# First attention of a two-layer macaron block: row maxima in halves of the heads, row sums out of the weighted sum

## What is computed

```python
disp, val = x @ w_disp + b_disp, x @ w_val + b_val          # per head 16 numbers
strain = disp_win - disp[:, :, :, None, :]                  # 32 earlier places per token
bond_act = gelu(strain @ w_strain + b_strain + state @ w_state_i + state_win @ w_state_j + rel_emb @ w_pos)
bond_logits = (bond_act @ w_bond_out)[..., 0] + b_bond_out[0]
damage_act = gelu(strain @ w_damage + b_damage)
damage = sigmoid((damage_act @ w_damage_out)[..., 0] + b_damage_out[0])
weights = softmax(where(cmask, bond_logits - damage * 10.0, -inf), axis=-1)   # over 32 places
out = einsum('bntd,bntde->bnte', weights, val_win)          # reshaped, then @ w_cproj + b_cproj
```

## Time and profile before

| | |
|---|---|
| median of 3 runs | 3083.24 us (3081.63 to 3083.78) |
| the profiled execution | 3079.87 us |
| its span, first to last instruction | 3078.1 us |
| around the span | 1.8 us |
| a0 within the span | 606.9 to 1311.9 us, chunks from 651.4 to 1263.2 |
| busy in the whole span: PE, DVE, ACT, POOL | 92%, 55%, 51%, 43% |
| one middle batch of a0 (1026.9 to 1106.3, 79.4 us), busy: PE, DVE, ACT, POOL | 70.6, 71.1, 72.3, 69.6 us |

### The profile page before, as it was taken

The page is one execution under the profiler, slowest core; times in us unless marked ns, Lnnn a source line. Parts: engine busy times, 40 slices in busy tenths (PEclk is TensorE's granted clock), DMA queues, the critical chain, the costliest instruction groups (busy, mean ns, idle before and its releaser), DMA issues. The chain is left out here.

```text
span 3078.1 us, 54231 instructions
## 1 busy us (share of the span) xinstructions
PE 2825.6 (92%) x19419; PEld 2033.0 (66%) x19419; DVE 1696.4 (55%) x4655; ACT 1562.0 (51%) x2621; POOL 1325.5 (43%) x1315
## 2 busy tenths in 40 slices
PE   6899999878988898788999998999789999988999
PEld 5799999733444443468999996666446666655666
DVE  5411111279888888673111111776776666656766
ACT  1133333359999898412333332333267777783333
POOL 5444444369888888363444442000134434320000
PEclk9899999979999999869999998999889999999999
DMA  8199999712222111363999997000142343301000
GB/s 288 60 324 330 325 328 328 221 52 62 63 59 63 53 56 48 97 217 113 329 324 324 325 325 215 1 0 0 49 111 73 87 100 97 80 1 40 14 14 20
DMA packets 299088, 432.11 MB, mean 140 GB/s; under 512 B 21185, under 2 KB 249702, under 8 KB 295782
## 3 DMA queue, kind: packets, MB, share of 16 engines
q1 hardware_dynamic: 273462, 394.66, 40.4%
q0 software_dynamic: 24576, 33.57, 5.1%
q10 hardware_dynamic: 816, 0.79, 0.1%
HBM read 356.08 MB, written 72.88 MB: 139 GB/s over the span
## 5 line engine op out<-in xcount | busy, mean ns | idle before, releaser
L1806 ACT ACTIVATE f_h_t<-f_h_ps,f_b_t 128x128 f32<-128x128 f32 x1024 | 321.8, 366 | 593.7 <-PE f_h_ps L1764 593.7
L2187 POOL TENSOR_TENSOR a_dmg_buf<-a_c 128x2048 f32<-128x2048 f32 x128 | 519.7, 4093 | 66.5 <-PE a_dmg_ps L2251 44.0
L1764 PEld LDWEIGHTS f_h_ps<-f_rows_t,f_w 128*128 128x128 f32 x4096 | 481.2, 193 | 9.9 <-issue 3.5
L1764 PE MATMUL f_h_ps<-f_rows_t,f_w 128*128 128x128 f32 x4096 | 482.4, 276 | 2.3 <-DVE f_rows_t L1820 1.2
L1778 PE MATMUL f_y_ps<-f_w,f_h_t 128*128 128x256 f32 x2048 | 483.4, 379 | 0.0
L1724 POOL DMA_INDIRECT acc_rows<-f_y,f_give x128 | 205.0, 1602 | 487.2 <-DMA acc_rows<-f_y,f_give 447.4
L1778 PEld LDWEIGHTS f_y_ps<-f_w,f_h_t 128*128 128x128 f32 x2048 | 369.8, 190 | 39.9
L1820 DVE COPY f_rows_t<-f_t_ps 128x256 f32<-128x256 f32 x128 | 54.3, 424 | 598.3 <-PE f_t_ps L1752 598.3
L2563 DVE SCALAR_TENSOR_TENSOR a_bond_buf<-a_a,a_small_rep,a_q_ps 128x512 f32<-128x512 f32 x512 | 346.8, 741 | 7.5 <-PE a_q_ps L2381 3.8
L999 ACT ACTIVATE a_prob<-a_prob,a_neg_top 128x384 f32<-128x384 f32 (+3 forms) x512 | 277.7, 572 | 46.7 <-POOL a_neg_top L816 46.4
L536 DVE SCALAR_TENSOR_TENSOR x_resid<-f_y_ps,f_gate,x_resid 128x256 f32 x512 | 217.1, 478 | 129.0 <-PE f_y_ps L384 120.0
(11 more groups left out here) (357 smaller groups left out, 4172.2 us busy)
## 6 DMA issues: line engine op xcount, KB each, us to landing
f_w<-in_L_ffn_w_dram SPq DMA_DIRECT2D x256, 1024.0 KB
a_skewed<-skew SPq DMA_DIRECT2D x32, 512.0 KB, 5.8
a_k_s<-parts SPq DMA_DIRECT2D x16, 768.0 KB, 7.7
acc_rows<-x_resid SPq DMA_DIRECT2D x17, 512.0 KB, 7.7
xn_rows<-f_xn SPq DMA_DIRECT2D x16, 512.0 KB, 3.6
a_vals<-val_rows SPq DMA_DIRECT2D x64, 128.0 KB, 2.8
skew<-a_bond SPq DMA_DIRECT2D x128, 64.0 KB, 1.7
x_resid<-acc_rows SPq DMA_DIRECT2D x30, 256.0 KB, 7.0
```

Of the source, the lines that this page charges most:

```text
L1764: last = nc.tensor.matmul(h_ps[n // HB][:, (n % HB) * P:(n % HB + 1) * P], w1_sb[s][:, c, n * P:(n + 1) * P], rows_t[e % 2][:, c, :], star ...
L1806: nc.scalar.activation(h_t[k][:, n, :], h_ps[n // HB][:, (n % HB) * P:(n % HB + 1) * P], ACT.Gelu, bias=b1_t[:, n, e:e + 1]).then_inc(gelu ...
L2187: nc.gpsimd.tensor_tensor(dmg_buf[n % RING][:, :, :], places(c_sb[h], first_place(dg)), c_sb[h][:, PAD:].unsqueeze(1).broadcast_to([P, DG, ...
```

## The change

The maxima and their subtraction are made for 8 heads at a time. The first half of a batch's heads has its logits after step 10 of the same batch, so its maximum is taken at step 11 and subtracted at step 12 of that batch; the second half keeps steps 3 and 4 of the next batch. The exponential stays whole, at step 6. `inverse_sums` goes. In its place each head's 16 values get a 17th column of ones (`VD = BD + 1`), so that the matmuls of `sums` deliver the sum of a token's weights as column 17; `divide` takes its reciprocal out of PSUM (16 numbers a token) and then multiplies. The rows of values in DRAM grow from 256 to 272 numbers, the two DMA reads of a tile from 512 to 544 bytes a row. Since `sums` now writes 272 columns of its bank, the transposed context and the projection change places in it.

```diff
-    TOP_Q, LESS_Q, EXP_Q, SUM_Q = 3, 4, 6, 8
+    TOP_Q, LESS_Q, EXP_Q = (11, 3), (12, 4), 6
...
-        inv_sum = [sb(f"inv_sum{k}", [P, TPB, NH]) for k in range(2)]
+        inv_sum = sb("inv_sum", [P, NH])
...
-        ctx_bank = lambda m: bond_ps[1][:, 0:D] if m >= LATE else o_ps[:, D:2 * D]
-        project_bank = lambda m: bond_ps[0] if m >= LATE else o_ps
+        ctx_bank = lambda m: bond_ps[1][:, 0:D] if m >= LATE else o_ps[:, 0:D]
+        project_bank = lambda m: bond_ps[0][:, 0:D] if m >= LATE else o_ps[:, D:2 * D]
...
+        def softmax_half(s, at):
+
+            i, now = divmod(s, STEPS)
+            if now == at[0] and i < B:
+                return i, 0
+            j = softmax_batch(s, at[1])
+            return None if j is None else (j, 1)
...
-                    first = val_dram[S - WIN + x * P:, r * HP * BD:]
-                    blocks = bass.AP(tensor=first.tensor, offset=first.offset, ap=[[D, SPAN], [WIN * D, BPT], [1, HP * BD]])
+                    first = val_dram[S - WIN + x * P:, r * HP * VD:]
+                    blocks = bass.AP(tensor=first.tensor, offset=first.offset,
+                                     ap=[[NH * VD, SPAN], [WIN * NH * VD, BPT], [1, HP * VD]])
...
-            def less_top(j):
-                for n, tiles in enumerate(soft_parts(j)):
+            def less_top(j, h):
+                heads = slice(h * HH, (h + 1) * HH)
+                for n, tiles in enumerate(half_parts(j, h)):
                     count = tiles.stop - tiles.start
-                    rows = bond[j % 2][:, tiles, :, :]
-                    pool.wait_ge(top_ready, j + n + 1)
-                    nc.gpsimd.tensor_tensor(rows, rows, top[:, tiles, :].unsqueeze(2).broadcast_to([P, count, WIN, NH]),
+                    rows = bond[j % 2][:, tiles, :, heads]
+                    pool.wait_ge(top_ready, HALF * j + h + n + 1)
+                    nc.gpsimd.tensor_tensor(rows, rows, top[:, tiles, heads].unsqueeze(2).broadcast_to([P, count, WIN, HH]),
                                             ALU.subtract).then_inc(soft_ready, 1)
...
-            def inverse_sums(j):
-                dve.wait_ge(exp_done, j + len(soft_parts(j)))
-                nc.vector.tensor_reduce(inv_sum[j % 2][:, :, :], bond[j % 2][:, :, :, :].rearrange("p j w h -> p j h w"),
-                                        AX.X, ALU.add)
-                nc.vector.drain()
-                nc.vector.reciprocal(inv_sum[j % 2][:, :, :], inv_sum[j % 2][:, :, :])
...
             def divide(m):
-                j, x = divmod(m, TPB)
-                if x == 0:
-                    nc.vector.drain()
+                summed = o_ps[:, 0:NH * VD].rearrange("p (h d) -> p h d", d=VD)
                 dve.wait_ge(out_ready, m + 1)
+                nc.vector.reciprocal(inv_sum[:, :], summed[:, :, BD])
                 if m:
                     dve.wait_ge(ctx_turned, m)
-                nc.vector.tensor_tensor(ctx_sb[:, :].rearrange("p (h d) -> p h d", d=BD),
-                                        o_ps[:, 0:D].rearrange("p (h d) -> p h d", d=BD),
-                                        inv_sum[j % 2][:, x, :].unsqueeze(2).broadcast_to([P, NH, BD]),
-                                        ALU.mult).then_inc(ctx_ready, 1)
+                nc.vector.drain()
+                nc.vector.tensor_tensor(ctx_sb[:, :].rearrange("p (h d) -> p h d", d=BD), summed[:, :, 0:BD],
+                                        inv_sum[:, :].unsqueeze(2).broadcast_to([P, NH, BD]), ALU.mult).then_inc(ctx_ready, 1)
```

More of the change, by code:

```diff
@@ L1867, in attn0_phase @@
     HP = NH // 2
+    VD = BD + 1
     RING = 3
@@ L2076, in softmax_batch, with half_parts @@
             i, now = divmod(s, STEPS)
-            if i == B and q > TOP_Q:
+            if i == B and q > TOP_Q[1]:
                 q -= 1
             return i - 1 if now == q and 0 < i <= B else None
+        def softmax_half(s, at):
[4 more added lines that the diff above has]
+            return None if j is None else (j, 1)
         def soft_parts(j):
             return [slice(x, x + 1) for x in range(TPB)] if j == B - 1 else [slice(0, TPB)]
+        def half_parts(j, h):
+            return soft_parts(j) if h else [slice(0, TPB)]
         @block.sync
@@ L2229, in _ @@
                     damage_chunk(s + 1)
-                j = softmax_batch(s, LESS_Q)
-                if j is not None:
-                    less_top(j)
+                soft = softmax_half(s, LESS_Q)
+                if soft is not None:
+                    less_top(*soft)
         @block.tensor
@@ L2333, in project @@
                 for c in range(DC):
[L2334 to L2335 removed]
+                    nc.tensor.matmul(project_bank(m), ctx_t[:, c, :], w_out_sb[:, c, :], start=c == 0, stop=False)
+                nc.tensor.matmul(project_bank(m), ones[:, :], b_out_rows[:, :], start=False, stop=True).then_inc(proj_ready, 1)
             def turn_tokens(i, c):
@@ L2522, in _ @@
             nc.scalar.activation(vals[:, :, :, :].rearrange("p b r n -> p (b r) n"),
-                                 core.ident[:, :].unsqueeze(1).broadcast_to([P, 2 * NBLK, HP * BD]), ACT.Copy,
+                                 core.tile(0, 0)[:, 0:HP * VD].unsqueeze(1).broadcast_to([P, 2 * NBLK, HP * VD]), ACT.Copy,
                                  scale=0.0).then_inc(vals_cleared, 1)
@@ L2592, in copy_logits, with find_top @@
                                         ALU.add).then_inc(logits_copied, 1)
-            def find_top(j):
+            def find_top(j, h):
+                heads = slice(h * HH, (h + 1) * HH)
                 if j:
-                    dve.wait_ge(soft_ready, j)
+                    dve.wait_ge(soft_ready, HALF * (j - 1) + h + 1)
                 nc.vector.drain()
-                for tiles in soft_parts(j):
-                    nc.vector.tensor_reduce(top[:, tiles, :], bond[j % 2][:, tiles, :, :].rearrange("p j w h -> p j h w"),
+                for tiles in half_parts(j, h):
+                    nc.vector.tensor_reduce(top[:, tiles, heads], bond[j % 2][:, tiles, :, heads].rearrange("p j w h -> p j h w"),
                                             AX.X, ALU.max).then_inc(top_ready, 1)
-            def inverse_sums(j):
-                dve.wait_ge(exp_done, j + len(soft_parts(j)))
-                nc.vector.tensor_reduce(inv_sum[j % 2][:, :, :], bond[j % 2][:, :, :, :].rearrange("p j w h -> p j h w"),
-                                        AX.X, ALU.add)
-                nc.vector.drain()
-                nc.vector.reciprocal(inv_sum[j % 2][:, :, :], inv_sum[j % 2][:, :, :])
             def copy_turned(m):
@@ L2646, in add_projected @@
                 dve.wait_ge(proj_ready, m + 1)
-                nc.vector.tensor_tensor(xt, project_bank(m)[:, 0:D], xt, ALU.add).then_inc(proj_added, 1)
+                nc.vector.tensor_tensor(xt, project_bank(m), xt, ALU.add).then_inc(proj_added, 1)
             def copy_tokens(i, c):
@@ L2818, in _ @@
                     copy_logits(g)
-                j = softmax_batch(s, TOP_Q)
-                if j is not None:
-                    find_top(j)
-                j = softmax_batch(s, SUM_Q)
-                if j is not None:
-                    inverse_sums(j)
+                soft = softmax_half(s, TOP_Q)
+                if soft is not None:
+                    find_top(*soft)
 def macaron(nc, t, out, phases="f0 a0 f0 f1 a1 f1"):
```

25 lines of the change are left out of this document (14 added, 11 removed).

## The result

The changed kernel takes 3057.97 us (median of 4 runs, 3054.57 to 3059.94) beside 3083.24 us of the kernel before (4 runs, 3081.63 to 3083.78): ratio 0.9918, 95% interval 0.9901 to 0.9935. The forecast was 3055 us. In two later comparisons it took 3053.8 and 3053.5 us beside 3082.5 and 3081.4: 0.9909 (0.9896 to 0.9923) and 0.9906 (0.9890 to 0.9921).

The account below looks back on a forecast made before the run. It took batches 2 to 6 as bound by hand-overs between in-order engines. Gains 20.1 + 3.0 + 4.5 - 0.7 + 0.8 = 27.7 off the profiled 3079.87, plus 3.37 to the median, gave 3055 us, range 3050 to 3062.

Parts of the forecast that it names:

- the end: Last batch's softmax chain: first maximum and first subtraction halve, less 0.35 for a reciprocal; 0.8 us gained.
- stretches from step 8 to 2, five: Bond GELU of step 8 to that of the next batch's step 2, batches 2 to 6: 45.0 us each, 20.1 gained.
- step 3, five batches: Halved maximum in step 3 makes DVE earlier and removes a wait of 0.57: 0.6 us a batch, 3.0 gained.
- batch 7: Last batch, no token work for a next: wait behind the maximum shrinks 1.8, that behind the sum goes; 4.5 us gained.
- batches 0 and 1: POOL has no idle time there, so the early subtraction was charged one more stall: 0.7 us lost.
- The sum goes, the half maximum comes: Step 8 loses its sum (4.28 us with its gap), step 11 gains a half maximum of 1.92, 2.0 with its gap.
- TensorE's wait for the second copy: Sign of being right: PE waits for the second copy of means, step 12, below 1 us.
- sign against the forecast: Sign of being wrong: new waits of ACT in steps 12 and 13 above 1 us.
- surplus of 1.3 us: Even batches' stretch was 49.5 us, odd 48.3; all five were taken at 45.0, since the excess came behind the sum.
- The clock: TensorE's clock, 0.79 of full behind step 9's idle 3.74 us, should become whole; if not, some 5 us come back.
- TensorE as the bound: Rival, chance 0.07: PE's own backlog sets step 2, so only 7.6 us are gained, 3075 us.

Follow-up runs that it names:

- the halves alone: Changed kernel with the whole sum of step 8 back and no column of ones, maxima and subtraction still by halves: 3081.28 us, 0.9997 of the kernel before.
- the ones alone: Changed kernel with maxima and subtraction whole again in steps 3 and 4, column of ones kept: 3063.4 and 3068.35 us, 0.9947 and 0.9953 of the kernel before.
- The two kernels with a longer maximum: Changed kernel with step 11's half maximum found again into a spare tile: all 1024 columns, 3080.71 us; only 512 columns, 3068.92 us.

## Why the prediction was right

The mechanism, the size and the place were right; all terms but the end came out within 1 us. Before and after, each from its profiles:

| term | forecast | measured |
|---|---|---|
| stretches from step 8 to 2, five | -20.1 | -20.9 (245.5 to 224.6) |
| step 3, five batches | -3.0 | -3.5 (0.70 each, step 2 to 8) |
| batch 7 | -4.5 | -4.4 (72.1 to 67.7) |
| batches 0 and 1 | +0.7 | +1.6 (135.2 to 136.8, mean of three) |
| end | -0.8 | -2.8 (55.4 to 52.5) |
| sum | -27.7 | -29.5 in the stage |

The measured terms together are 0.5 over the stage's 29.5, and batch 2 loses 0.4 of it in its first steps. That the total came so close to 3055 is in part luck: the stage gained 1.8 us more than forecast, the part ahead of it was 2.4 shorter in the profiles and the part behind it 3.9 longer, and neither was in the sum.

*The sum goes, the half maximum comes.* The stretch takes 44.83 to 44.86 us in four batches and 45.20 in the last, forecast 45.0. From the bond GELU of step 8 the second copy of means starts at 20.8 us as forecast (1088.3 in the old time), `a` at 21.6 for a forecast of 21.4, the bond GELU of step 14 stands 3.5 us earlier for 3.6. Half maximum 1.94 (1.92), reciprocal 0.25 (0.25), subtraction 2.36 (2.4), TensorE's wait for the second copy 0.74 (below 1). The wait of 1.69 us that ACT has in step 13 is no sign against the forecast: it was 1.62 before. That the even batches lose their surplus of 1.3 us was an assumption and came true; the clock says where it went.

*The clock.* I had it in the sum, as a row at the lower level in step 9, and it fell in more places than that one. Batch 4 of before and of after beside batch 5 of the earlier trace rows:

```profile
946.00:1026.90 80.90, 72.82 (x686) 33.43 (x686) 71.24 (x111) 72.32 (x47) 69.67 (x18) 0.94 0.20 59
```
```profile
937.10:1012.30 75.20, 69.22 (x686) 32.03 (x685) 67.90 (x113) 71.79 (x47) 69.61 (x19) 1.00 0.22 65
```

The granted clock was 0.94 in the long, even batches and 0.98 in the odd ones (in the second profile of before batch 2 had 0.96 and was 0.5 us shorter); in the changed kernel it is 1.00 in all five, and they are alike. The same goes together elsewhere: with the halves alone the stretch from step 8 to 2 is 49.1 to 49.3 us in the batches at 0.98 and 50.3 in the two at 0.96, and with the ones alone the one batch at 0.96 is over 1 us longer than those at 0.98. So the surplus of the even batches goes with the clock, which the forecast took away with the sum without naming it. The two kernels with a longer maximum show the price of a fall by itself: 1.6 us. The exact share of the clock in the gain stays open: I did not take the sum away at a held clock.

*TensorE as the bound* had 0.07. As a statement on the whole gain it is wrong, but it is the limit that comes next, some 0.5 us behind. Without any maximum in the stretch it takes 44.3 us in most batches (the ones alone) and with it 44.86. That TensorE waits for the second copy of means, so that DVE's way is the critical one, was right for anything longer and wrong for anything shorter: 1.95 us moved off that way brought nothing, 1.95 us more on it cost 3.5.

*The mis-sized terms.* The end was short by 2. Its first subtraction starts 13.6 us behind the last bond GELU (14.6 before), the DMAs 15.0 (16.5), the turn on TensorE 28.6 (30.8): I counted the maximum and one subtraction, and not the writes and reads behind them (8.20 us for 8.52) nor that the remaining turns are shorter too. Batches 0 and 1 were short by 0.9: I priced one stall of POOL at 0.7 and saw it in batch 0, and the runs put most of the loss at the end of batch 1. One step later for the early halves and there is none (135.2). Which engine's wait makes the difference stays open.

*The small price of the halves.* The forecast priced both edits together, and had no term for the wait of step 5 that the halves shorten. The runs part them: the ones bring 25 us of the stage and the halves on top of them 4.7. The halves alone bring 3 of the stage and nothing that can be measured in the total.

## What to carry to other kernels

A piece of work is worth its length only where its engine is the last to arrive: the same maximum of 1.9 us cost 0.5 us in a stretch where another engine was late, and 3.5 where its engine was (1.9 of its own, 1.6 of TensorE's clock), so find out by how much the next engine lags before moving more. Make a sum that a matmul can carry along in a spare column; here it made them 34 columns wide instead of 32 and took 3.7 us off the engine that was waited for. And when a small edit moves a stage that it doesn't touch, look at the packets of the instruction queue in that stage before looking for a mechanism.

## What the runs showed of the hardware

- Where code lies can cost more than what it does. With the ones alone, the first pass of `f1` fetched 19 packets of instructions in place of 4, ScalarE waited 4.2 to 4.6 us for VectorE in three turns of the loop, and the pass took 313 to 315 us instead of 306 to 308. Eight idle groups of instructions ahead of it removed this.
- The clock at nearly the same idle time of TensorE, 1.70 and 1.68 us, once stayed and once fell; after waits of 1.65 and 1.66 in batches 0 and 1 of the changed kernel the two rows of matmuls took 1.12 to 1.13 and 1.02, at the full clock; after 2.57 the clock stood at 0.54. A wait of 2.01 us in step 5 was followed by a fall in the even batches of the kernel before and not in the odd ones. A fall cost 1.6 us where it was parted from the rest.
- A reduction in this strided pattern takes 0.58 us for 256 columns, 1.02 for 512, 1.94 for 1024 and 3.73 for 2048: a straight line in the columns.
- The subtraction on GpSimd took 2.37 us in runs of 8 for half the columns, 4.59 in runs of 16 for all: the length of the run cost about 3%.
